# A three-pass graph kernel: weight matrices per source block kept in DRAM, and eleven gather-free runs instead of nine in the second pass

## The reference, cut to what matters

```python
def gcn_conv(x, src, dst, ew, W, b):
    deg = segment_sum(ew, dst, n)
    dinv = where(deg > 0, rsqrt(deg), 0.0)
    norm = dinv[src] * ew * dinv[dst]
    out = segment_sum((x @ W)[src] * norm[:, None], dst, n)
    return out + b
# edges and one self loop of weight 1 for each node
x = layernorm(x + sigmoid(gcn_conv(relu(gcn_conv(x, W1, b1)), W2, b2)))
# then one attention layer over the same edges, with r_h = edge_attr (E x 128):
z = x @ fc_w.T;  rh = r_h @ fc_r_w.T
e = leaky_relu(z[src] @ a0 + z[dst] @ a1 + rh @ a2)
alpha = segment_softmax(e, dst)
out = layernorm(x + relu(segment_sum(alpha[:, None] * (z[src] + rh), dst) + z @ loop_w))
```

## Time and profile before

| | |
|---|---|
| time, median of 3 runs | 2405.95 us (2403.78 to 2406.47) |
| span of the profiled execution | 3348.6 us |
| busy in it: PE / DVE / POOL / ACT | 2044.2 / 1834.8 / 1718.9 / 946.7 us |
| mean granted TensorE clock | 0.787 of 2.4 GHz |
| DMA | 270.54 MB, mean 81 GB/s |

### The profile page before, as it was taken

How to read it: one execution, slowest core, us unless ns; L and a number is a source line. 1 busy time by engine, 2 the same in 40 slices (tenths; PEclk the granted TensorE clock), 3 DMA queues, 4 the chain that set the end, 5 groups by cost and what they waited for, 6 DMA issues and landing times.

```text
span 3348.6 us, 40819 instructions
## 1 busy us (share of the span) xinstructions
PE 2044.2 (61%) x13384; PEld 1762.3 (53%) x13384; DVE 1834.8 (55%) x7005; ACT 946.7 (28%) x1754; POOL 1718.9 (51%) x1781
## 2 busy tenths in 40 slices
PE   1416444588888911177777888106677667756786
PEld 1315433566767811166666677005666666645675
DVE  3626435577779810156656687217654564546457
ACT  1316000122233300033333444101254225412541
POOL 7351666665550067466556500555766646663640
PEclk9857667798999955588988899557778778877888
DMA  4112221222221122123333332525343534443431
GB/s 118 30 42 66 69 61 47 61 61 63 60 62 32 51 76 53 41 74 86 99 103 102 93 91 80 138 62 147 97 103 97 134 93 102 108 117 79 103 97 34
DMA packets 272093, 270.54 MB, mean 81 GB/s; under 512 B 43454, under 2 KB 218709, under 8 KB 271862
## 3 DMA queue, kind: packets, MB, share of 16 engines
q1 hardware_dynamic: 201790, 143.87, 15.1%
q0 software_dynamic: 56640, 117.52, 14.8%
q10 hardware_dynamic: 13448, 6.47, 0.7%
HBM read 254.14 MB, written 13.97 MB: 80 GB/s over the span
## 4 chain that ended last, share of the span: by engine, by line
PE 35%; DVE 21%; another core or an unknown queue 21%; issue 15%; ACT 4%; SPq 1%; DMA 1%; POOL 1%; ACTq 0%; DVEq 0%; POOLq 0%
PE ps L858 9%; PE ps L910 8%; DVE SR L1608 5%; PE ps L860 3%; PE ps L898 3%; PE ps L1045 2%; DVE U L1709 2%; DVE SR L1681 2%; DVE SR L1571 1%; PE ps L885 1%; DVE U L1648 1%; PE ps L1029 1%; POOL ring L720 1%; PE ps L792 1%
## 5 line engine op out<-in xcount | busy, mean ns | idle before, releaser
L720 POOL DMA_INDIRECT ring<-x_d,srcC x1132 | 1109.7, 980 | 971.2 <-issue 579.0
L858 PE MATMUL ps<-SR,ring 128*128 128x128 f32 x3540 | 672.5, 320 | 205.0 <-issue 132.0
L858 PEld LDWEIGHTS ps<-SR,ring 128*128 128x128 f32 x3540 | 580.5, 231 | 238.9 <-issue 178.9
L720 POOL DMA_INDIRECT ring<-h_d,srcC x494 | 469.9, 951 | 457.1 <-DMA h_d<-Lb 170.9
L1681 DVE TENSOR_SCALAR SR<-iota_r,cols 128x288 f32<-128x288 f32 x735 | 365.0, 564 | 303.9 <-remote 226.6
L910 PE MATMUL ps<-SR 128*128 128x288 f32 x1470 | 416.6, 435 | 118.1 <-ACT SR L1232 75.3
L910 PEld LDWEIGHTS ps<-SR 128*128 128x128 f32 x1470 | 292.3, 205 | 212.7 <-ACT SR L1232 77.5
L860 PE MATMUL ps<-SR 128*128 128x128 f32 x1564 | 340.3, 312 | 40.8 <-issue 34.6
L1232 ACT COPY SR<-ps 128x512 f32<-128x512 f32 (+1 forms) x195 | 106.0, 561 | 758.4 <-remote 502.9
L860 PEld LDWEIGHTS ps<-SR 128*128 128x128 f32 x1564 | 279.6, 228 | 48.3 <-issue 48.0
L898 PE MATMUL ps<-rows,SR 128*128 128x128 f32 x1470 | 196.2, 285 | 122.5 <-ACT SR L1241 90.6
(11 more groups left out here) (288 smaller groups left out, 2703.4 us busy)
## 6 DMA issues: line engine op xcount, KB each, us to landing
SR<-in_edge_attr_dram SPq DMA_DIRECT2D x97, 512.0 KB
SR<-low_d SPq DMA_DIRECT2D x90, 256.0 KB
U<-dlo_d SPq DMA_DIRECT2D x74, 256.0 KB
ring<-x_d,srcC POOLq DMA_INDIRECT x1132
ring<-h_d,srcC POOLq DMA_INDIRECT x494
SR<-dlo_d SPq DMA_DIRECT2D x12, 512.0 KB
ring<-in_edge_attr_dram SPq DMA_DIRECT2D x12, 512.0 KB
U<-lo_d SPq DMA_DIRECT2D x18, 256.0 KB
```

What stands on the lines that cost most here:

```text
L720: pool.indirect_dma_start(ring[:, ring_at(p, h if p < 2 else q), k, 0:width], None, (x if p == 0 and h < R0 else table)[:, :], bass.Indire ...
L858: last = nc.tensor.matmul(ps[(p * NA + k) % 2][:, at], ring[:, ring_at(p, h), j, 0:D], S[:, gg % NS, j, :], start=False, stop=stop)
```

## The change

It changes how a set is used in passes 0 and 1, how many sets there are, and the order of some steps.

- **Product the other way round.** `build_pair` multiplies one-hot block (now 128x128 from `iota` and `slotL` on ACT, without a load from DRAM) and slot matrix (128x288) into a 128x288 weight matrix per source block; ACT copies it to SBUF block by block (`copy_blocks`); `sum_slots` multiplies `rows[:, a]` by it. A built block so costs two products of 128x288 in place of one of 128x128 and one of 128x288.
- **Kept.** In pass 0 SP stores each chunk of these matrices (up to 128 x 1152 float32) to `b_d` in DRAM (`store_mat`), 78 chunks. In pass 1 the six sets that pass 0 used are loaded again (`load_mat`, four buffers) and are neither made by DVE and ACT nor built by PE; the other five are built.
- **Eleven runs in pass 1** in place of nine, so 54 groups with gathers in place of 62. Both new sets are sorted in pass 0, one set each five steps instead of six.
- `low_d` and `load_low` go, but for the three sets that pass 2 uses. `NQ` is 11, and a slot is free once built from. `make_ranks` stands ahead of `make_hi` and `build_S`; the products of the builds are placed around `count_before`, the picks and `add_sets`; picks go up to four a step; `node_table` of one bank is later.
- Semaphores of the path for odd inputs (`wide_...`), which is not run here, are merged.

```diff
-SETK = (6, 8, 10, 12, 14, 15, 2, 4, 9)
-USED = ((0, 1, 2, 3, 4, 5), (6, 7, 0, 1, 8, 2, 3, 4, 5))
+SETK = (6, 8, 10, 12, 14, 15, 2, 3, 5, 9, 13)
+USED = ((0, 1, 2, 3, 4, 5), (6, 7, 8, 0, 1, 9, 2, 3, 10, 4, 5))
-NQ = 15
+NQ = 11
+NBT = (3, 4)
+BCH = 4 * NARROW
-MAKE = [17 + 6 * i for i in range(NSET)]
+EFFORT = [7 if RUNS[N0 + m // NC] in USED[0] else 10 for m in range(len(USED[1]) * NC)]
+CHUNK_AT = [[29 + m * 40 // (N0 * NC) for m in range(N0 * NC)], [1 + sum(EFFORT[:m]) // 24 for m in range(len(USED[1]) * NC)]]
+MAKE = [17 + 5 * i for i in range(NSET)]
...
+            def store_mat(m):
+                sp.wait_ge(s("looked_copied"), slot_no(m, buckets(m)[-1]) + 1)
+                sp.dma_start(b_d[m, :, 0:len(buckets(m)) * NARROW], mat(m)).then_inc(mat_moved[place_of(m)], 16)
+            def load_mat(m):
+                if holder(m) is not None:
+                    sp.wait_ge(s("slot_summed"), slots_to(holder(m)))
+                sp.dma_start(mat(m), b_d[kept(m), :, 0:len(buckets(m)) * NARROW]).then_inc(mat_moved[place_of(m)], 16)
...
-            def look_up(m):
...
+            def build_pair(m, half):
+                for i, a in [*enumerate(buckets(m))][2 * half:2 * half + 2]:
...
+                    if n >= 2:
+                        pe.wait_ge(s("looked_copied"), n - 1)
+                    nc.tensor.matmul(ps[3 + n % 2][:, 0:NARROW], ohB[:, built_chunk(m) % 2, i * P:(i + 1) * P], slotS[:, n % NQ, :], start=True, stop=True
+                                     ).then_inc(s("looked"), 1)
+            def sum_slots(m):
+                if not is_built(m):
+                    pe.wait_ge(mat_moved[place_of(m)], 16 * moves_to(m))
...
-                    nc.tensor.matmul(ps[5][:, SLACK:SPAN], rowX[:, m % 2, i * P:(i + 1) * P], slotS[:, n % NQ, :], start=False, stop=a == NB - 1
+                    nc.tensor.matmul(ps[5][:, SLACK:SPAN], rows[:, a, 0:D], mat(m)[:, i * NARROW:(i + 1) * NARROW], start=False, stop=a == NB - 1
...
+            def copy_blocks(m):
...
+                    nc.scalar.copy(mat(m)[:, i * NARROW:(i + 1) * NARROW], ps[3 + n % 2][:, 0:NARROW]).then_inc(s("looked_copied"), 1)
...
+            def slot_onehot(c):
...
+                for i, a in enumerate(buckets(m)):
+                    nc.scalar.activation(ohB[:, c % 2, i * P:(i + 1) * P], iota[:, :], ACT.Abs, bias=slotL[:, s_, a:a + 1]).then_inc(s("low_apart"), 1)
...
+                nc.scalar.activation(ohB[:, c % 2, 0:w], ohB[:, c % 2, 0:w], ACT.Relu, bias=negp[:, 1:2], scale=-1.0).then_inc(s("oh_made"), 1)
```

More of the change, by code:

```diff
@@ L140, in slots_to, with is_built, slot_no, built_chunk @@
     return m // NC * NB + buckets(m)[-1] + 1
+def is_built(m):
+    return m // NC in BUILT
+def slot_no(m, a):
+    return BUILT.index(m // NC) * NB + a
+def built_chunk(m):
+    return BUILT.index(m // NC) * NC + m % NC
+def place_of(m):
+    return m % NBT[0] if m < N0 * NC else (m - N0 * NC) % NBT[1]
+def holder(m):
+    return m - NBT[0] if m < N0 * NC else m - NBT[1] if m - NBT[1] >= N0 * NC else None
+def kept(m):
+    return USED[0].index(RUNS[m // NC]) * NC + m % NC
+def stores_of(j):
+    return len(range(j, N0 * NC, NBT[0])) if j < NBT[0] else 0
+def moves_to(m):
+    return stores_of(place_of(m)) + sum(not is_built(i) and place_of(i) == place_of(m) for i in range(N0 * NC, m + 1))
+def summed_at(m):
+    return CHUNK_AT[1][m - N0 * NC] + 1
 def made_at(h, after):
@@ L428, in build @@
         low_loaded = [sem(f"low_loaded{j}") for j in range(2)]
+        mat_moved = [sem(f"mat_moved{j}") for j in range(NBT[1])]
         h1_stored = [sem(f"h1_stored{j}") for j in range(2)]
@@ L454, in closed, with mat, await_mats_stored @@
             return AT[p] + CLOSEH[p][k] + 1
+        def mat(m):
+            return mats[place_of(m)][:, 0:len(buckets(m)) * NARROW]
+        def await_mats_stored(eng):
+            for j in range(NBT[0]):
+                eng.wait_ge(mat_moved[j], 16 * stores_of(j))
         def stored(sems, k):
@@ L580, in _ @@
             load_dlo(1)
+            await_mats_stored(sp)
+            for m in range(N0 * NC, N0 * NC + NBT[1]):
+                if not is_built(m):
+                    load_mat(m)
             for h in range(HS[1] + 4):
@@ L603, in _ @@
                         sp.dma_start(x2_d[b0 * P:b1_ * P, :].rearrange("(b p) d -> p b d", p=P), preX[:, k % 2, 0:b1_ - b0, :]).then_inc(x2_stored[k % 2], 16)
+                for m in range(N0 * NC + NBT[1], len(RUNS) * NC):
+                    if not is_built(m) and summed_at(holder(m)) == h:
+                        load_mat(m)
             for i in range(REST + 1 + NP_DLO, G // 2):
@@ L967, in _ @@
                     sum_slots(m)
+                for s_, g in made_at(h, 2):
+                    if g == ST // GT - 1 and s_ in XR:
+                        turn_low(s_)
                 for k in range(NA):
@@ L972, in _ @@
             for h in range(HS[1]):
-                for m in chunks_at(1, h - 1):
-                    look_up(m)
+                pairs = [(m, half) for m in chunks_at(1, h - 1) if is_built(m) for half in range(2)]
+                for m, half in pairs[:len(pairs) // 2]:
+                    build_pair(m, half)
                 for q in picks_at(h - 1):
@@ L977, in _ @@
                 add_sets(1, h)
+                for m, half in pairs[len(pairs) // 2:]:
+                    build_pair(m, half)
                 sum_group(1, h)
@@ L1356, in far_onehot @@
                 if m >= 2:
[L1357 removed]
+                    act.wait_ge(s("looked"), K0 + m - 1)
                 if kind == PERM:
@@ L1731, in _ @@
                     select(h)
+                for s_, g in made_at(h, 1):
+                    make_ranks(s_, g)
                 for s_, g in made_at(h, 0):
```

237 lines of the change are left out of this document (116 added, 121 removed).

## The result

The kernel after takes 2606.76 us (median of 4 runs, 2601.71 to 2611.53) against 2406.21 us before (4 runs, 2403.78 to 2409.91): 1.083 times as long, interval 1.081 to 1.086, or +200.6 us. The forecast was 2498 us, +92, with 2340 to 2580 as its range. The direction was right; 109 us are missing.

The account below looks back on a forecast made before the run. The prediction took PE to set the pace in passes 0 and 1, with gathers close behind. Its terms, +79 + 24 + 49 - 60 = +92 us, took 2405.95 us to 2498 us, with a range of 2340 to 2580 us.

Parts of the forecast that it names:

- wider products: Pass 0, PE: 294 look-ups of 128x128 become products of 128x288, +79 us.
- eight more groups of sorting: Pass 0, PE: two more sets to sort, permuting 1.92 us and counting 1.10 us a group, +24 us.
- more PE work: Pass 1, PE: built and kept sets take 419 us against 352, +67 us; eight groups less give -18 us.
- waits given back: Pass 1: PE's waits for S and one-hots, 60.3 us, all go; bounds were all or none.
- I take nothing: Pass 0: `make_ranks` moved ahead of `build_S` counted as 0; bounds 40.2 us back or 11 us more.
- The price of builds and sorting in pass 0: Pass 0: wider products and eight more groups of sorting cost PE +103 us together.
- Still nothing: Pass 0: ACT's copies of built blocks, 0.472 us against PE's 0.534 us over two PSUM banks, cost 0.
- The doubt about the gathers: 1770 gathers take 2212 us, 92% of 2405.95; rivals: gathers pace pass 1 alone (0.17) or both passes (0.27).
- POOL still waits for line 858: Sign for pass 0 with sets: POOL goes on waiting for PE's `sum_group` in the changed profile.
- The likeliest case: PE sets the pace in both passes: chance 0.48, 2498 us, own range 2440 to 2560 us.
- The transfers: 43.4 MB stored in pass 0 and loaded in pass 1, a chunk landing in some 2 us: hidden, 0.
- Cold builds: Rival: pass 0's 588 set products paced by copies at a lower clock, +122 us; chance 0.08 shared with late loads.

Follow-up runs that it names:

- e6: The kernel after with the nine sets of before, sorted each six steps, and DVE's order of before in pass 0: 2480.98 us, ratio 1.0306.
- e2: The kernel before with eleven sets sorted each five steps, only nine of them used: 2434.52 us, ratio 1.011.
- e5: The kernel after with DVE's order of before in pass 0 (`make_hi`, `build_S`, `make_ranks`): 2536.9 us, ratio 1.0535.
- e7: The kernel before with `make_ranks` ahead of `make_hi` and `build_S` in pass 0, nothing else: 2470.55 us, ratio 1.0266.
- e11: The kernel before with DVE's order in pass 0 `build_S`, `make_ranks`, `make_hi`: 2405.74 us, ratio 0.9995.
- e13: The kernel after with DVE's order in pass 0 `build_S`, `make_ranks`, `make_hi`, nothing else: 2564.72 us, ratio 1.0654.
- e1: The kernel after with the nine sets of before, sorted each six steps: 2505.22 us, ratio 1.040.
- e8: The kernel before with each look-up of pass 0 multiplied twice on PE: 2432.14 us, ratio 1.0108.
- e14: The kernel after with most of ACT's copies of built blocks cut from 288 to 72 columns: 2580.92 us, ratio 1.0722.
- e9: The kernel before with each look-up of pass 1 multiplied twice on PE: 2435.46 us, ratio 1.0116.
- e10: The kernel before with PE's count of a group of sorting moved behind `sum_group`: 2375.52 us, ratio 0.985.
- e4: The kernel after with stores and loads of kept matrices in `b_d` cut to 16 columns: 2605.15 us, ratio 1.0825.

## Why the prediction was wrong in size

By steps, in us of the profiled spans (+204.5 in all) beside the forecast:

| | forecast | measured | from |
|---|---|---|---|
| pass 0: wider products | +79 | +70 | e6, end of pass 0 |
| pass 0: eight more groups of sorting | +24 | +26 | e2, and e5 against e6, end of pass 0 |
| pass 0: moved ranks | 0 | +74 | after against e5 |
| pass 1: more PE work | +67 -18 | +50 busy | windows |
| pass 1: waits given back | -60 | -23 idle | windows |
| pass 2 and between | 0 | +8 | table above |

- **The step that failed** is "I take nothing" for the order of `make_ranks`, `make_hi` and `build_S`. Its bounds, -40 to +11, looked only at the wait that the trace already had, PE's for the ranks. I didn't ask what is queued behind `make_ranks` on its new place: `build_S`, for which `sum_group` waits in every step, and that `make_ranks` itself waits for PE's `permute` of the same step. In before the order costs 66 us (e7), all of it S (e11); in after it costs 70 (e5), of which 42 are S (e13); with nine sets and kept matrices it costs 24 (e6 against e1). About half of the 70 is idle time of PE; in the other half the same products take longer, at a lower granted clock. Without the order the kernel takes 2536.9 us, inside the forecast's range.
- **The price of builds and sorting in pass 0** was right, +96 against +103, each of its two terms near its forecast. That the sum held was in part luck: it left out that PE's wait ahead of the count would be filled (45.6 us in before, 12.0 in e5) and that builds would bring waits of their own (29.2 us in e5, for copies and slots), and these two are of about one size. A build's product also takes more than assumed. PE's groups in steps 29 to 69 of after, to be held against the earlier trace rows:

```profile
L953 PE MATMUL ps<-SR 128*128 128x288 f32 x588 | 182.6, 435 | 29.5 <-ACT SR L1303 26.8 <-DVE SR L1765 2.0
L966 PE MATMUL ps<-SR,rows 128*128 128x288 f32 x586 | 150.0, 408 | 0.0
```

 182.6 / 294 = 0.621 us for a built block, 0.510 for the plain product, where 0.534 was taken for both. The 104.9 us of busy time in these steps are not the measure of the sum: with the old order (e5) they are 86.9. And PE time doesn't always count in full: of e8's 50 us of busy time 25 lengthened pass 0.
- **"Still nothing" for the copies** was wrong: it compared 0.472 us of ACT with 0.534 of PE, but a build, its copy and the next build in the same bank follow on each other. PE waits 26.8 us for them in steps 29 to 69, and thinner copies gave 26 us in the two passes (e14).
- **Pass 1** had the right work (+49 forecast, +50 measured) and a credit that was too large. The waits for S and one-hots went, as forecast, but PE's idle time fell by 23 us and not by 60: waits for copies took their place, and the pass had been paced by its gathers, so that idle time of PE was slack. e1 takes 143 us off DVE there and gains nothing. An estimate from e9: 61 us of idle time is what PE has at its densest there, which would give 573.7 + 61 = 634 us; 666 were measured, 16 of the difference are copies (e14), and the other 16 are open. The other moves in this pass (picks, `node_table`, the place of the builds) were not tried alone.
- **The doubt about the gathers** was right in half. Pass 1 of before was paced by them; pass 0, whose last gather ends 35 us before its last sum, wasn't until e10 freed it. The 115.4 us that POOL waited for line 858, the evidence against, are only in the first profile: in the second POOL doesn't wait for it in pass 1, and 0.6 us in steps 29 to 69. So the sign "POOL still waits for line 858" failed too, with 1.2 us. The likeliest case didn't weigh enough that this profile was 942.65 us too long in more than its holes.
- **The transfers** are hidden, as forecast (e4), though a chunk took 5.3 us from issue to landing, not 2 (loads into `Lb`, the only ones with a figure). The Trainium skill (DMA: Bandwidth & Descriptors, Measured) gave an estimate of 3.6 us for such a chunk, nearer but still short of the trace; the page counts the busy time of the DMA engines alone.
- **Cold builds** didn't come: the clock in steps 29 to 69 was 0.96. But a lower clock cost time elsewhere: it fell to 0.70 in steps 18 to 28, where PE stood waiting in a stretch with no builds. The rule weighed ahead of the result (the Trainium skill, TensorE: Matmul & The Clock Gate, A second HAM failure mode: psum-queue depth-cycling) was not borne out for the builds themselves: they wait for banks, and the clock stays.
- **A slip in the sum**: 40 us below 2498 is 2458, so the likeliest case's own range should have begun there, not at 2440.

Along one path from before to after the 200 us divide so, by the ratios: sorting two more sets each five steps +26 (e2), building, keeping and using eleven sets +102 (e5 against e2), the order +72 (after against e5). Building and keeping with only nine sets is +74 (e6), nearly all of it in pass 0: the kept matrices cost there and, in a pass 1 paced by gathers, gave nothing back.

## What to carry to other kernels

When a step is moved on an in-order engine, list what it waits for and what now stands behind it; a wait that looked free delays all that is queued behind it, here 66 us for two lines. Count the clock too: where TensorE is made to stand, the same products can take longer afterwards. Before a wait counts as a gain, ask what would end the idle time next: an engine's waits in a pass that is paced by another are no credit. If a profiled span is far above the measured time, take it again before reading shares and who waits for whom from it.

## What the runs showed of the hardware

- One profiled execution of the same kernel had a span of 3348.6 us and another 2404.3; the first showed PE busy for 219 us more and a ring full for 80.1 us, which the second doesn't have.
- 72 us of products added to a PE that was 87% busy at a clock of 0.93 gave 50 us of busy time at 0.98 and 25 us of length.
- After PE had stood for 2.95 us in e7, the granted clock was 0.53 from 375.0 to 378.6 us against 1.00 from 367.0 to 371.0, and eight float32 products of 128x128 by 128x128 took 3.57 us in place of 1.98.
- 43.4 MB stored and 43.4 MB loaded in chunks of 576 KB, with 0.35 and 0.48 of the DMA engines' time in use: cutting them to 16 columns changed the time by under 2 us (e4).
